# The start of a macaron transformer block on one core: the instruction orders of the first two phases laid anew

## The reference

```
x = x + 0.5 * ffn(layernorm(x))          # ffn: layernorm with gamma, beta; ternary 256x256 weight; bias
x = x + attention(layernorm(x))          # 16 query heads, 4 key/value heads, 128 wide, rope,
                                         # causal window of 64, softmax, output product and bias
x = x + 0.5 * ffn(layernorm(x))
```

## Time and the profile before

| what | value |
|---|---|
| median of 3 runs | 811.15 us |
| the profiled execution | 812.07 us |
| its span, first to last instruction | 810.2 us |
| TensorE busy | 787.2 us (97%) |
| VectorE, ScalarE, GpSimd busy | 640.0, 515.1, 449.9 us |
| mean granted TensorE clock | 0.994 |

### The profile page before, as it was taken

The page is one execution under the profiler, slowest core; times in us unless marked ns, Lnnn a source line. Parts: engine busy times, 40 slices in busy tenths (PEclk is TensorE's granted clock), DMA queues, the critical chain, the costliest instruction groups (busy, mean ns, idle before and its releaser), DMA issues.

```text
span 810.2 us, 16063 instructions
## 1 busy us (share of the span) xinstructions
PE 787.2 (97%) x5678; PEld 734.2 (91%) x5678; DVE 640.0 (79%) x1294; ACT 515.1 (64%) x1633; POOL 449.9 (56%) x435
## 2 busy tenths in 40 slices
PE   7899999999999999999999999999999999999984
PEld 6689999999999999999999999999999999999984
DVE  5888868888788877888779786888878887787644
ACT  5377765676657665676656766567666666574662
POOL 4577736575465644566446664556546564464532
PEclk9999999999999999999999999999999999999997
DMA  8464224442342424323234332444234242424300
GB/s 296 117 159 96 50 53 106 103 99 45 67 119 66 110 49 105 91 66 92 53 91 104 89 71 53 105 104 98 44 74 113 66 112 47 104 53 105 79 2 26
DMA packets 52431, 70.53 MB, mean 87 GB/s; under 512 B 7040, under 2 KB 30080, under 8 KB 52352
## 3 DMA queue, kind: packets, MB, share of 16 engines
q1 hardware_dynamic: 52064, 69.43, 35.2%
q10 hardware_dynamic: 288, 0.08, 0.0%
HBM read 10.76 MB, written 4.19 MB: 18 GB/s over the span
## 4 chain that ended last, share of the span: by engine, by line
PE 86%; DVE 5%; ACT 2%; issue 2%; POOL 2%; DMA 2%; SPq 0%; ACTq 0%; POOLq 0%
PE job_p L572 29%; PE attn_p L572 22%; PE scores_p L588 12%; PE heads_p L572 11%; PE probsT_p L626 6%; PE job_p L698 4%; PE job_p L687 2%; ACT headsT L942 1%; DVE headsT L762 1%; DMA q_s<-wk 1%; ACT probs L920 1%; DVE parts L842 1%; POOL q_s L1046 1%; DVE variance L851 1%; DMA rope_swap<-rope_sin 1%
## 5 line engine op out<-in xcount | busy, mean ns | idle before, releaser
L1026 POOL TENSOR_TENSOR probs<-probs,inv_sum 128x512 f32<-128x512 f32 x128 | 134.4, 1050 | 197.5 <-DVE inv_sum L756 197.3
L920 ACT ACTIVATE probs<-scores_p,neg_max 128x128 f32<-128x128 f32 x512 | 181.0, 372 | 52.4 <-DVE neg_max L750 51.8
L572 PE MATMUL attn_p<-wo_s,headsT 128*128 128x256 f32 x1536 | 208.9, 285 | 5.3 <-DVE headsT L762 5.3
L572 PE MATMUL job_p<-xnT,wq_s 128*128 128x512 f32 x768 | 204.9, 403 | 1.9 <-DVE v_s L794 1.8
L572 PEld LDWEIGHTS attn_p<-wo_s,headsT 128*128 128x128 f32 x1536 | 195.5, 191 | 11.7 <-DVE headsT L762 7.3
L1046 POOL TENSOR_TENSOR q_s<-rope_cos,rope_swap 128x512 f32<-128x512 f32 x128 | 164.4, 1292 | 54.4 <-DMA rope_swap<-rope_sin 54.3
L942 ACT ACTIVATE headsT<-heads_p,columns_s 128x512 fp32r<-128x512 f32 x128 | 88.2, 689 | 154.3 <-PE heads_p L572 152.8
L572 PEld LDWEIGHTS job_p<-xnT,wq_s 128*128 128x128 f32 x768 | 135.9, 189 | 26.9 <-DVE v_s L794 2.7
L762 DVE SCALAR_TENSOR_TENSOR headsT<-heads_p,columns_s,headsT 128x512 fp32r<-128x512 f32 x128 | 95.7, 748 | 59.6 <-ACT headsT L942 58.2
L588 PE MATMUL scores_p<-k_s,q_s 128*128 128x128 f32 x1024 | 135.2, 275 | 0.4 <-POOL q_s L1046 0.4
L588 PEld LDWEIGHTS scores_p<-k_s,q_s 128*128 128x128 f32 x1024 | 125.8, 192 | 2.5 <-POOL q_s L1046 0.9
(11 more groups left out here) (73 smaller groups left out, 925.3 us busy)
## 6 DMA issues: line engine op xcount, KB each, us to landing
rope_swap<-rope_sin SPq DMA_DIRECT2D x320, 128.0 KB, 2.3
v_odd<-v_s SPq DMA_DIRECT2D x64, 192.0 KB, 3.3
x_in<-x SPq DMA_DIRECT2D x16, 256.0 KB, 3.3
out<-x_res SPq DMA_DIRECT2D x16, 256.0 KB, 2.5
staging<-wo SPq DMA_DIRECT2D x2, 512.0 KB, 10.5
staging<-wq SPq DMA_DIRECT2D x2, 512.0 KB, 10.7
x_res<-wo SPq DMA_DIRECT2D x2, 512.0 KB, 3.8
x_res<-wv SPq DMA_DIRECT2D x1, 512.0 KB, 7.3
```

The costliest lines, as they stand in the source:

```text
L572: mm = nc.tensor.matmul(dst, a(p), b(q), start=first and clears and i == 0, stop=last and i == 2, skip_group_check=True)
L920: ins = nc.scalar.activation(probs[:, i, k, :], scores_p[i][:, k, :], ACT.Exp, bias=neg_max[:, i, k:k + 1], accum_out=row_sum[:, i, k:k + 1])
L1026: nc.gpsimd.tensor_tensor(probs[:, i, :, :], probs[:, i, :, :], inv_sum[:, i, :].unsqueeze(2).to_broadcast([P, 4, P]), ALU.mult).then_inc( ...
```

## The change

The orders of prologue and first phase are laid anew on all five engines. What moves:

- VectorE's prologue has w0 and w5 ahead of XT0, w2 behind it and w4 behind XT1 (before: w2, w1, w0, w4 ahead of XT0, w3 behind it, w5 behind XT1). YT0 stands ahead of the folding of beta.
- GpSimd takes w3 and w1 as well as w6 and w8, all four ahead of its rope additions K0 and Q0 to Q3. Its w3 waits until VectorE's w5 is done.
- TensorE's beta stands behind YT1. fill0 and fill1 use a tile of ones in place of the identity, so they don't wait for the identity's load; FILLS changes from (3, 3, 2, 2, 4, 4) to (10, 3, 5, 2, 4, 4, 12), and the last, fill6, stands in the epilogue between YT0p and YT1p.
- ScalarE takes YT0 ahead of norm1, both anorm ahead of XT0, w6 ahead of V00 and w8 behind it, w7 and mask1 behind V01.
- The second half of batch 0's x is loaded from ScalarE's queue, first of all, not from SP's. On SP, stage8i goes behind the ten rope swaps of the prologue, load0n ahead of K1c's swaps, and stage9f behind K2c's.
- total waits for two semaphores, ones_set and abs_summed, that were one.
- The first phase's orders differ in the places of neighbouring steps.

The diff; the first phase's orders are left out but for SP's:

```diff
--- before.py
+++ after.py
@@ -57,17 +57,17 @@
 
 TENSOR = {
     "prologue": """
-        fill0i total0i fill1i YT0n fill2i beta0i YT1n fill3i FO0n FO1n open0i fill4i XT0n fill5i
+        fill0i total0i fill1i YT0n fill2i YT1n beta0i FO0n fill3i FO1n open0i fill4i XT0n fill5i
         XT1n V00n K0n Q0n Q1n Q2n Q3n V01n
     """,
...
@@ -88,22 +88,22 @@
         T14c
     """,
     "epilogue": """
-        O13p W14p T15p O14p W15p O15p YT0p YT1p FO0p FO1p
+        O13p W14p T15p O14p W15p O15p YT0p fill6p YT1p FO0p FO1p
     """,
 }
 VECTOR = {
     "prologue": """
-        ones0i stats0n stats1n tern0i beta0i YT0n YT1n FO0n astats0n FO1n astats1n w2i w1i w0i
-        w4i XT0n w3i XT1n w5i V00n K0n Q0n Q1n Q2n Q3n V01n
+        ones0i stats0n stats1n tern0i YT0n beta0i YT1n FO0n astats0n FO1n astats1n w0i w5i XT0n
+        w2i XT1n w4i V00n K0n Q0n Q1n Q2n Q3n V01n
     """,
...
@@ -130,16 +130,16 @@
 }
 SCALAR = {
     "prologue": """
-        abs0i norm0n norm1n w2i YT0n YT1n w5i w3i w4i w0i w6i w1i anorm0n mask0n
-        XT0n anorm1n XT1n w8i V00n mask1n w7i V01n
+        abs0i norm0n YT0n norm1n YT1n w2i w5i w0i w3i w1i w4i mask0n anorm0n anorm1n
+        XT0n XT1n w6i V00n w8i V01n w7i mask1n
     """,
...
@@ -162,13 +162,14 @@
 }
 GPSIMD = {
     "prologue": """
-        scale0n scale1n half0i bias0n bias1n ascale0n ascale1n w6i w8i K0n Q0n Q1n Q2n Q3n
+        scale0n scale1n half0i bias0n bias1n ascale0n ascale1n w3i w6i w8i w1i K0n Q0n Q1n
+        Q2n Q3n
     """,
...
@@ -187,10 +188,10 @@
 }
 SYNC = {
     "prologue": """
-        stage8i K0n Q0n Q1n Q2n Q3n shift0n
+        K0n Q0n Q1n Q2n Q3n stage8i shift0n
     """,
     "first": """
-        K1c Q4c Q5c Q6c stage9f Q7c load0n K2c Q8c Q9c Q10c Q11c shift1c K3c
+        load0n K1c Q4c Q5c Q6c Q7c K2c stage9f Q8c Q9c Q10c Q11c shift1c K3c
         Q12c Q13c Q14c Q15c K0n Q0n Q1n Q2n Q3n shift0n
     """,
@@ -207,7 +208,7 @@
 }
 
 
-FILLS = (3, 3, 2, 2, 4, 4)
+FILLS = (10, 3, 5, 2, 4, 4, 12)
 PARTS = {"p": -1, "c": 0, "n": 1}
 WAVES = ("YT", "FO", "stats", "scale", "norm", "bias")
 
@@ -342,6 +343,7 @@
         split_lo_dve = sem("split_lo_dve")
         split_lo_pool = sem("split_lo_pool")
         v_shifted = sem("v_shifted")
+        ones_set = sem("ones_set")
         abs_summed = sem("abs_summed")
         scale_ready = sem("scale_ready")
         thr_step = sem("thr_step")
@@ -548,7 +550,6 @@
 
             load_half(0, 0)
             sp.dma_start(w_full[:, :, :], ffn_wT.rearrange("(c p) n -> p c n", p=P)).then_inc(tern_in, 16)
-            load_half(0, 1)
             sp.dma_start(rows_s[:, :, :], rows.partition_broadcast(P)).then_inc(rows_in, 16)
             for n in range(3):
                 stage(sp, n)
@@ -702,7 +703,8 @@
 
             def sum_scale(_):
 
-                pe.wait_ge(abs_summed, 2)
+                pe.wait_ge(ones_set, 1)
+                pe.wait_ge(abs_summed, 1)
                 nc.tensor.matmul(probsT_p[:, 0, 0:1], ones, thr[:, 0:1],
                                  start=True, stop=True).then_inc(scale_ready, 1)
 
@@ -725,9 +727,12 @@
 
             def fill(x):
 
-                pe.wait_ge(ident_in, 16)
+                pe.wait_ge(ones_set, 1)
+                square = ones if x[1] < 2 else identf[:, :]
+                if x[1] >= 2:
+                    pe.wait_ge(ident_in, 16)
                 for _ in range(FILLS[x[1]]):
-                    nc.tensor.matmul(flat_heads(heads_p[:, :])[:, 0:P], identf[:, :], identf[:, :], start=True, stop=True)
+                    nc.tensor.matmul(flat_heads(heads_p[:, :])[:, 0:P], square, square, start=True, stop=True)
 
             for x in PE_STEPS:
                 {"S": scores, "T": transpose_probs, "W": values, "O": project, "K": rope_job, "Q": rope_job,
@@ -863,7 +868,7 @@
                                         x_res[:, 2 * m:2 * m + 2, :], ALU.add).then_inc(attn_read, 1)
 
             def set_ones(_):
-                nc.vector.memset(ones, 1.0).then_inc(abs_summed, 1)
+                nc.vector.memset(ones, 1.0).then_inc(ones_set, 1)
 
             def ternary(_):
 
@@ -990,6 +995,7 @@
                                                scale=gamma_s[:, e:e + 1])
                 ins.then_inc(ln_hi, 1)
 
+            act.dma_start(x_in[:, 2:4, :], x_t[0][:, 2:4, :]).then_inc(x_loaded[1], 16)
             act.dma_start(identf[:, :], ident).then_inc(ident_in, 16)
             act.dma_start(columns_s[:, :], columns).then_inc(columns_in, 16)
             act.wait_ge(power_ready, 1)
@@ -1006,6 +1012,9 @@
                 n = x[1]
                 _, where, dst = PIECES[n]
                 pool.wait_ge(split_hi, HIGH[x] + 1)
+                if n == 3:
+
+                    wait_split(pool, 5)
                 nc.gpsimd.tensor_tensor(dst[1], where, dst[0].bitcast(F32), ALU.subtract).then_inc(split_lo_pool, 1)
 
             def scale_of(x):
```

More of the change, by code:

```diff
@@ L63 @@
     "first": """
[L64 to L70, removed]
+        K1c Q4c Q5c S0c S1c Q6c V10c T0c Q7c S2c W0c T1c S3c K2c
+        O0c W1c T2c Q8c S4c Q9c O1c W2c V11c T3c S5c Q10c O2c W3c
+        T4c S6c Q11c O3c YT0n W4c T5c K3c O4c W5c S7c Q12c T6c YT1n
+        O5c FO0n S8c W6c Q13c T7c S9c O6c Q14c W7c FO1n T8c Q15c O7c
+        XT0n W8c S10c T9c XT1n S11c O8c W9c K0n T10c S12c O9c Q0n W10c
+        T11c V00n S13c O10c W11c T12c Q1n S14c Q2n O11c W12c Q3n T13c S15c
+        O12c V01n W13c T14c
     """,
@@ L95 @@
     "prologue": """
-        ones0i stats0n stats1n tern0i beta0i YT0n YT1n FO0n astats0n FO1n astats1n w2i w1i w0i
-        w4i XT0n w3i XT1n w5i V00n K0n Q0n Q1n Q2n Q3n V01n
+        ones0i stats0n stats1n tern0i YT0n beta0i YT1n FO0n astats0n FO1n astats1n w0i w5i XT0n
+        w2i XT1n w4i V00n K0n Q0n Q1n Q2n Q3n V01n
     """,
     "first": """
[L100 to L106, removed]
+        K1c Q4c Q5c max0c max1c inv0c Q6c inv1c w11f probsT0c V10c max2c Q7c heads0c
+        inv2c probsT1c K2c max3c probsT2c heads1c max4c inv3c Q8c stats0n Q9c stats1n inv4c heads2c
+        max5c probsT3c V11c Q10c inv5c heads3c max6c probsT4c Q11c inv6c w12f heads4c probsT5c K3c
+        YT0n max7c heads5c Q12c YT1n probsT6c inv7c max8c FO0n heads6c astats0n Q13c probsT7c inv8c
+        max9c Q14c heads7c FO1n inv9c astats1n probsT8c Q15c max10c heads8c XT0n probsT9c XT1n inv10c
+        max11c heads9c max12c probsT10c inv11c K0n inv12c Q0n heads10c probsT11c max13c V00n heads11c inv13c
+        probsT12c max14c Q1n Q2n heads12c max15c inv14c probsT13c Q3n inv15c V01n
     """,
@@ L132 @@
     "prologue": """
-        abs0i norm0n norm1n w2i YT0n YT1n w5i w3i w4i w0i w6i w1i anorm0n mask0n
-        XT0n anorm1n XT1n w8i V00n mask1n w7i V01n
+        abs0i norm0n YT0n norm1n YT1n w2i w5i w0i w3i w1i w4i mask0n anorm0n anorm1n
+        XT0n XT1n w6i V00n w8i V01n w7i mask1n
     """,
     "first": """
[L137 to L142, removed]
+        w11f exp0c exp1c mask2c mask3c probsT0c V10c heads0c exp2c probsT1c mask4c probsT2c heads1c exp3c
+        w9f w12f exp4c mask5c mask6c heads2c w10f probsT3c V11c exp5c norm0n heads3c probsT4c exp6c
+        norm1n heads4c probsT5c mask7c YT0n heads5c mask8c exp7c YT1n mask9c probsT6c heads6c exp8c probsT7c
+        heads7c exp9c probsT8c anorm0n mask10c mask11c anorm1n heads8c XT0n probsT9c XT1n exp10c mask12c heads9c
+        probsT10c exp11c exp12c heads10c mask13c mask14c probsT11c V00n exp13c heads11c mask15c probsT12c heads12c exp14c
+        probsT13c exp15c mask0n V01n mask1n heads13c
     """,
@@ L164 @@
     "prologue": """
-        scale0n scale1n half0i bias0n bias1n ascale0n ascale1n w6i w8i K0n Q0n Q1n Q2n Q3n
+        scale0n scale1n half0i bias0n bias1n ascale0n ascale1n w3i w6i w8i w1i K0n Q0n Q1n
+        Q2n Q3n
     """,
     "first": """
[L168 to L171, removed]
+        w7f probs0c K1c probs1c Q4c Q5c Q6c probs2c Q7c probs3c w9f K2c probs4c scale0n
+        scale1n Q8c Q9c probs5c w10f probs6c bias0n Q10c Q11c K3c residual0c probs7c bias1n probs8c
+        Q12c ascale0n probs9c ascale1n Q13c Q14c Q15c probs10c probs11c probs12c K0n Q0n probs13c Q1n
+        Q2n probs14c Q3n probs15c
     """,
```

## The result

| kernel | median, us | executions |
|---|---|---|
| before | 811.45 (810.39 to 812.33) | 7 |
| changed | 808.25 (807.06 to 809.28) | 7 |

The ratio is 0.9962, 95% interval 0.9951 to 0.9973: 3.1 us less, between 2.2 and 4.0 (the medians differ by 3.2). The forecast was 808.1. The steps that led to it are another matter. That the total came out this close is in part luck: the first FFN's wave gained where a loss had been put down, and the first phase and the end gave less than put down, and these errors cancel.

A forecast was written before the change was run, and what follows sets the result against it. TensorE's own rate was taken to bound 45 to 780 us, with waits only at the two ends. The terms -2.0 + 0.25 + 0 + 0 - 1.3 = -3.05 us gave 808.1 from the median 811.15; range 806.8 to 810.4.

The forecast's parts named there:

- Part 1: Prologue weight pieces, reordered on VectorE and partly moved to GpSimd: Q0, and S0c with it, 2.0 us earlier.
- A: End of anorm1 on ScalarE, 21.53 us in the kernel before; the prologue's later times are counted from it.
- the 1.8 us of cover: Prologue: margin between GpSimd's last rope addition, put at A + 14.9, and S0c, put at A + 16.75.
- Part 2: Wave of the first FFN in the prologue, with new orders, fills and x load: +0.25 us, bounds -0.8 and +1.2.
- X: Start of the first statistics on VectorE, 4.12 us before the change; 4.4 was taken for after it.
- F: Start of VectorE's residual addition of FO0, 14.85 us before; put between 14.0 and 16.0, taken as 15.1.
- Part 3: Loads moved on SP, stage8i behind Q3's swaps: cost 0, with 0.6 us of cover ahead of exp0c.
- Part 4: First phase's orders, neighbouring steps swapped: nothing to win, a loss of 0 to 0.5 us possible, 0 taken.
- Part 5: fill6p in the epilogue's idle hole: the clock doesn't fall, YT1 and FO1 run faster, -1.3 us.
- The rivals: Five: clock falls anyway 0.2, first FFN late 0.2, w4 loses turn 0.1, late load 0.04, GpSimd's queue sets S0c 0.06.
- w4's or w2's lost turn: Prologue rival: VectorE's w4 waits for GpSimd's w6, gain of Part 1 falls to 0.4, time 809.7; chance 0.1.
- the load: Rival: load behind SP's swaps lands late, w11f holds exp0c and T0c, 812.8 us or more; chance 0.04.

The follow-up runs named there:

- e4: The kernel before with only the weight pieces moved, ScalarE's order and stage8i's load to match: 809.08 us, ratio 0.9972 to before.
- e2: The changed kernel without fill6 between YT0p and YT1p: 808.70 us, ratio 0.9965 to before.
- e6: The changed kernel with beta ahead of YT1 on TensorE: 807.71 us, ratio 0.9953 to before.
- e8: The changed kernel with ScalarE's w6 ahead of XT0: 810.49 us, ratio 0.9985 to before.
- e10: The changed kernel with the first phase's orders of before and beta ahead of YT1: 806.68 us, ratio 0.9935 to before.
- e9: The changed kernel with stage8i's load ahead of the rope swaps on SP again: 813.86 us, ratio 1.0026 to before.
- e1: The kernel before with only fill6 added between YT0p and YT1p: 810.14 us, ratio 0.9988 to before.
- e12: The changed kernel measured again, with no edit: 808.19 us, ratio 0.9954 to before.

## Why the prediction was right, and where it wasn't

**Part 1, -2.0: right.** Q0 at A + 4.40 (4.3 put down, so 1.9 us earlier), w5 in 0.95 us, K0 then Q0 without a hole, and the 12.45 us behind unchanged. e4 measures 2.3 us for this part by itself. GpSimd's last rope addition ended at A + 15.7, not A + 14.9, and the 1.8 us of cover took that.

**Part 2, +0.25 (bounds -0.8 and +1.2): wrong in sign.** The working up to YT0 holds: X is 4.43, and the chain from there is as written. What failed is the choice of F, 15.1, "since the new fills start at 1 us but pause from 3.8". The ten fills don't pause at 3.8. The profile counts 20 matmuls for them, two to a fill, and they last until 5.66, 1 us short of total; the earlier trace rows had it already, where fill3, two fills, is four matmuls in 0.65 us. The faster pace is then there by YT0 in six executions of ten. The same fills left it out in e2, e6 and e8, so what decides isn't found. F averages 14.5 against 15.4 for the old wave: -0.9, just beyond the bound of -0.8; against the 14.85 that the prediction started from it is -0.4. e10 has F another 1.2 us earlier with beta ahead of YT1.

**Part 3, 0: right in the changed kernel, with thin cover.** The load landed 0.8 us later than put down, and 0.7 us of cover were left. That the step was needed at all (5.7 us in e9) wasn't worked out.

**Part 4, 0: mis-sized.** The prediction allowed a loss of 0 to 0.5 us and took 0. The traces give 0.6, the times 1.5 with an interval nearly as wide. The sign that TensorE would have no gap behind S0c failed, at T0c and at one output product.

**Part 5, -1.3: right in mechanism, its size not sharp.** Against the profile of before it is 1.3, against e4's 1.5, against e2's 0.7; by the times 1.0 (e1) and 0.5 (e2). The count was off here as well: twelve fills are 24 matmuls, 2.84 us instead of the 1.56 of twelve times 0.13, and leave a hole of 1.26, not 2.4 us. That probably made the outcome surer than was thought: the last output products leave holes of up to 1.6 us without the clock falling there. In the seven executions of the changed kernel and the eleven of e1 the mean granted clock is 0.997 to 1.000, against 0.994 to 0.998 in the 23 of the kernel before that ran beside e1. The mean doesn't say where a fall lies: the lower means of e9 (0.995 to 0.998) and e12's 0.998 go with falls at 36 and 8 us.

**The sum.** By the runs part 1 is -1.9, part 2 -0.4 to -0.9, part 4 +0.6 and part 5 -0.7 to -1.5, together -2.4 to -3.7. Measured -3.1, put down -3.05. An early first wave paid for the first phase. The terms by themselves are no surer than half a microsecond each, so the agreement to 0.05 us is no proof of them.

**The rivals.** Of the five none happened in the two profiled executions of the changed kernel. Two were brought about: w4's or w2's lost turn (e8) and the load (e9, in another form than foretold, through the swaps and not through w11f).

## What to carry to other kernels

Two engines whose operations take turns, as VectorE's splits and GpSimd's pieces do here, should be given their long pieces in an order in which one is done when the other starts; an operation behind the blocked one on the same queue pays for it too, and the part of the change that kept them apart was the one large item here (e4). Fill a hole before a chain's last matmuls with work nobody reads, and count in the profile how many instructions a fill really is. When several orders are laid anew at once, measure them by phase: here the start and the end gave the gain and the first phase, if anything, gave a little back, which the total hid.

## What the runs showed of the hardware

- A VectorE operation with two SBUF inputs of 256 columns took 0.42 us alone and 1.60 us when issued 1.04 us into a GpSimd operation of 2.36 us; it ended 0.28 us after it. 768 columns: 0.95 alone, 2.52 and 2.92 behind such an operation.
- A matmul of two float32 squares by this program (the fills on the identity or on ones) is two records, each 0.23 to 0.27 us at the slower pace and 0.12 to 0.16 at the faster, by how many stand in a row. The clock row stands at 1.00 through the first 12 us in the profiles of before, the changed kernel and e2, yet the same four transposes take 1.11, 0.66 and 1.06 us there: it shows a fall (e12), not the slower pace that an execution begins with.
- In the same hole of 3.9 us at the end the granted clock fell 2.9 and 2.8 us after the last matmul in two executions (before, e4) and 4.1 us after it in another (e2), and there came back in the middle of an eight-matmul product. In e9's hole of 3.7 us it fell after 3.1 us, and K1 then took 2.93 us instead of 1.58.
- A hole much shorter than that was followed by a fall too: in e1's profile TensorE was idle for 1.97 us ahead of FO0 and the clock fell at 14.3 us, 0.3 us into the product; in the kernel before a hole of 1.56 us ahead of the last output product was followed by none.
